# Attention and mixture-of-experts layer on one core: the stores of expert block results issued by SyncE instead of ScalarE

## The reference

```python
# x: 16 x 512 x 256
x = layernorm(x + attention(x))          # 16 heads of 16, rotary positions, ALiBi bias, softmax over 512 keys
shared = silu(X @ sW1 + sb1) @ sW2 + sb2
activation = sqrt(softplus(X @ routing_W.T + expert_bias))   # 8 experts
top_vals, top_idx = top_k(activation, 2)
y[e] = silu(X @ rW1[e] + rb1[e]) @ rW2[e] + rb2[e]           # hidden width 128
x = layernorm(x + shared + sum over the 2 chosen e of top_val * y[e])
```

## Time and profile before

| what | value |
|---|---|
| time, median of three runs | 1673.09 us (1669.12 to 1676.26) |
| the profiled execution's own time | 1669.12 us |
| its span, first to last instruction | 1667.3 us |
| granted TensorE clock, mean | 0.937 of full speed |
| busy: PE, DVE, ACT, POOL | 1458.2, 1173.1, 1018.0, 724.0 us |
| stores of block results | 77, first at 636.6 us, last at 1529.0 us |

### The profile page before, as it was taken

The page is one execution under the profiler, slowest core; times in us unless marked ns, Lnnn a source line. Parts: engine busy times, 40 slices in busy tenths (PEclk is TensorE's granted clock), DMA queues, the critical chain, the costliest instruction groups (busy, mean ns, idle before and its releaser), DMA issues.

```text
span 1667.3 us, 33130 instructions
## 1 busy us (share of the span) xinstructions
PE 1458.2 (87%) x11110; PEld 801.1 (48%) x11110; DVE 1173.1 (70%) x2631; ACT 1018.0 (61%) x1742; POOL 724.0 (43%) x655
## 2 busy tenths in 40 slices
PE   8888999999999988999989999998888888887467
PEld 4433444444444434554545544454455555564345
DVE  7765788877878786666666777768776567645584
ACT  1465666676766655767676666665566676675232
POOL 2233363554535354433425353625366343245730
PEclk8898999999999988999999999999999999998788
DMA  7444243434334243454545343444557566676531
GB/s 207 129 122 137 81 135 106 134 102 121 118 114 124 93 128 121 148 170 145 161 144 186 104 124 97 140 147 135 177 178 231 179 203 193 197 233 216 169 106 51
DMA packets 185349, 242.00 MB, mean 145 GB/s; under 512 B 67239, under 2 KB 104190, under 8 KB 185182
## 3 DMA queue, kind: packets, MB, share of 16 engines
q1 hardware_dynamic: 162138, 188.52, 37.5%
q0 software_dynamic: 10752, 29.37, 5.5%
q10 hardware_dynamic: 12292, 21.99, 3.7%
HBM read 152.53 MB, written 91.44 MB: 146 GB/s over the span
## 4 chain that ended last, share of the span: by engine, by line
PE 49%; SPq 18%; DVE 13%; DMA 11%; issue 6%; POOL 2%; ACT 1%; POOLq 0%; ACTq 0%; DVEq 0%
PE pS L644 13%; PE pV L686 9%; PE pG L710 5%; DVE negm L935 5%; SPq L390 3%; DMA d_rec<-scr 3%; PE pG L719 3%; DMA xg<-d_x 3%; PE pG L732 2%; SPq L459 2%; PE pG L821 2%; PE pG L813 2%; PE pS L650 2%; SPq L484 2%; SPq L393 2%
## 5 line engine op out<-in xcount | busy, mean ns | idle before, releaser
L935 DVE TENSOR_REDUCE negm<-pS 128x1 f32<-128x512 f32 x1024 | 659.1, 683 | 329.8 <-PE pS L650 323.2
L1371 ACT ACTIVATE ee<-pT,slp 128x512 f32<-128x512 f32 x1024 | 648.4, 684 | 213.5 <-PE pT L671 210.3
L644 PE MATMUL pS<-ka,qa 62*128 62x512 f32 x1024 | 480.0, 504 | 80.5 <-DVE negm L935 67.5
L665 PE MATMUL pT<-qa,ka 64*128 64x512 f32 x1024 | 477.7, 501 | 0.2 <-ACT ee L1371 0.2
L644 PEld LDWEIGHTS pS<-ka,qa 62*128 62x128 f32 x1024 | 196.8, 192 | 328.9 <-issue 312.9
L686 PE MATMUL pV<-ee,vv 128*32 128x512 f32 (+1 forms) x2048 | 288.0, 635 | 0.0
L650 PE MATMUL pS<-mAB,tri 64*128 64x64 bf16 x2048 | 242.3, 200 | 0.0
L671 PE MATMUL pT<-mAB,tri 64*128 64x64 bf16 x2048 | 239.1, 198 | 0.0
L1555 POOL TENSOR_TENSOR raw<-raw,rope 128x512 f32<-128x512 f32 x61 | 78.3, 1283 | 326.6 <-DVE sh L969 326.5
L665 PEld LDWEIGHTS pT<-qa,ka 64*128 64x128 f32 x1024 | 194.6, 190 | 4.7 <-issue 3.3
L650 PEld LDWEIGHTS pS<-mAB,tri 64*128 64x128 bf16 x2048 | 119.0, 99 | 136.9 <-issue 103.8
(11 more groups left out here) (186 smaller groups left out, 2227.3 us busy)
## 6 DMA issues: line engine op xcount, KB each, us to landing
d_part<-parts SPq DMA_DIRECT2D x63, 512.0 KB, 2.9
qa<-d_part SPq DMA_DIRECT2D x378, 64.0 KB
wb<-in_wb SPq DMA_DIRECT2D x77, 256.5 KB
xg<-d_x SPq DMA_DIRECT2D x77, 256.0 KB, 2.8
d_y<-yb ACTq DMA_DIRECT2D x77, 256.0 KB, 3.2
ka<-d_part SPq DMA_DIRECT2D x128, 128.0 KB
xT<-in_xT SPq DMA_DIRECT2D x16, 512.0 KB, 4.0
ka<-d_part SPq DMA_DIRECT2D x128, 64.0 KB
```

What stands on the lines that cost most here:

```text
L644: e.matmul(pS[:, k, :], qa[g % 4][r, i, t * 128:t * 128 + 128].bitcast(F32R), ka[g % 4][r, i, :].bitcast(F32R), start=True, stop=False)
L665: e.matmul(pT[:, k, :], ka[g % 4][r, i, kt * 128:kt * 128 + 128].bitcast(F32R), qa[g % 4][r, i, :].bitcast(F32R), start=True, stop=False)
L935: e.tensor_reduce(negm[:, g % 2, j, t + k:t + k + 1], pS[:, k, :], AX, ALU.max, negate=True).then_inc(s_max, 1)
L1371: e.activation(ee[:, k, d % 7, :], pT[:, k, :], ACT.Exp, scale=slp[:, 6, h:h + 1]).then_inc(s_exp, 1)
```

## The change

`store_block` moves from ACT's program to SP's, unchanged. In a step, SP issues it behind the loads of a block and ahead of the writes of rotated queries and keys; ACT issued it behind the two exponentials and ahead of everything else. The step (B+4), the wait for the copy, the tile and the count of landings stay.

```diff
@@ SyncE's program
+        def store_block(q):
+            g = GROUP_OF_BLOCK[q]
+            j = q - FIRST_BLOCK[g]
+            e.wait_ge(g_free[bk("downb", 0, q)], full("downb", 0, q))
+            e.dma_start(d_y[g][j * ROWS:(j + 1) * ROWS, :].rearrange("(p k) c -> p k c", k=2), yb[q % 3][:, :, :]
+                        ).then_inc(y_w[q % 3], 16)
...
             for q in LOAD_BLOCKS.get(s, ()):
                 load_block(q)
+            if (q := block_due(s, STOREB)) >= 0:
+                store_block(q)
@@ ScalarE's program
-        def store_block(q):
-            g = GROUP_OF_BLOCK[q]
-            j = q - FIRST_BLOCK[g]
-            e.wait_ge(g_free[bk("downb", 0, q)], full("downb", 0, q))
-            e.dma_start(d_y[g][j * ROWS:(j + 1) * ROWS, :].rearrange("(p k) c -> p k c", k=2), yb[q % 3][:, :, :]
-                        ).then_inc(y_w[q % 3], 16)
...
             if 0 <= s - LAG < NC:
                 exps(s - LAG)
-            if (q := block_due(s, STOREB)) >= 0:
-                store_block(q)
```

## The result

The changed kernel takes 1682.95 us, the median of twelve (1677.53 to 1693.48). The kernel before, run twelve times beside it, takes 1670.86 (1661.7 to 1676.26). The ratio is 1.0083, with a 95% interval of 1.0055 to 1.0111: slower by 0.8%, about 14 us. (The quotient of these two medians is 1.0072, or 12 us; the ratios of this document are the recorded ones, and the two ways of counting differ by up to 0.2%.) The forecast was 1683.5 and +0.6%.

A forecast was written before the change was run, and what follows sets the result against it. PE leads the chain with 49%, SyncE's queue holds 18%, ACT 1%. 0 from ACT + 8.0 for issues + 2.4 for queueing = +10.4 us on the median 1673.09: 1683.5 us, +0.6%, range 1673 to 1698.

The forecast's parts named there:

- ACT gets back nothing: On ACT, a store's 0.33 us of queue is covered by the running 0.67 us exponential, so 0 is gained.
- SP pays 0.40 us for an issue: On SP's queue, each moved store takes 0.40 us, priced from SP's own plain write of a tile.
- 20 places on the chain, 8.0 us: Of 77 stores, 20 fall where the chain runs through SP, four in 744-850 us, sixteen later: 8.0 us.
- the second rival: SP's slack runs out, so every store counts: bound +40 us, case +20, 1693 us; chance 0.16.
- The queue, 2.4 us: Stores ahead of three reciprocal writes, and the last store behind an output write, delay landings 0 to 1.2 us each: 2.4.
- Later stores, 0: SP's later stores delay group 1's first gather and the reuse of store tiles: cost 0, at most about 1 us.
- The store's line is on the chain: Sign: the store's line appears on the chain some twenty times at about 0.4 us.
- SPq's share: Sign: the share of the chain held by SyncE's queue rises from 18%.
- PE's wait for tokens: Sign: PE's wait for a block's tokens grows from 49.3 us by roughly the sum; 20 us or more means slack ran out.
- The waits for DVE in the first stretch: Sign: SP's waits for DVE between 640 and 940 us, its slack there, shrink.
- Relief (3): SP's round trips from 1195 to 1530 us shorten, 21.6 us back: -13.6, 1659.5 us; chance 0.07 shared with ACT being held.
- Paid back (1): Loads and round trips on the chain land sooner, 4.1 us back, no queue term: +3.9, 1677 us; chance 0.33.

The follow-up runs named there:

- experiment 1: Against the kernel before, an unused register read added at each of the 77 store places: on SP ratio 1.0109, on ACT 0.9978.
- Experiment 8: Against the kernel before, ACT also issues softmax-sum writes, outputs, the weight row's read and loads of weights and bias: 1665.94 against 1683.27 us, ratio 0.9899.
- Group 0 alone: SP issues only the 31 stores of group 0, ACT the others; against the kernel before 1686.79 against 1683.27 us, ratio 1.0045.
- experiment 5: Stores split between SP and ACT, against the kernel before: SP with group 0 (31 stores) ratio 1.0045, SP with groups 1 and 2 (46) ratio 1.0110.
- experiment 3: Kernel before, stores still on ACT but two steps later for the first 55 blocks and one step later for the rest: ratio 0.9978.

## Why the prediction was right, point by point

- **Sign and size: right.** +0.6% was forecast, +0.83% and +0.86% measured. That 1683.5 us is only 0.5 from the measured 1682.95 is luck: the median of before that I started from lies 2.2 us above that of twelve, and the step that I added is 2 to 4 us too small.
- **ACT gets back nothing: confirmed.** The starts are unchanged, and 0.45 us more per place on ACT's queue costs nothing measurable (experiment 1). Experiment 8 shows the condition: it holds while what the queue does fits under the running exponentials.
- **SP pays 0.40 us for an issue: confirmed** by the fences above (0.40 to 0.46). That SP's time alone is enough for such a loss is shown by the register read, which moves nothing; scaled to 0.40 us it gives 0.6% of the 0.83%.
- **20 places on the chain, 8.0 us: the term that was mis-sized.** The two profiles have 29 and 34, 14.0 and 14.5 us. I had laid the stores onto the chain of before; but where PE led with SP close behind, the added 0.40 us can let SP take the lead. That is my reading of the extra places, and it is the second rival's mechanism, at about a third of its bound of 40 us: SP's waits for DVE and ACT held enough slack for the rest. The prediction counted only the two waits for DVE in the first stretch and overlooked the 23.7 us for ACT. Of the stores on the chain 9 and 5 are in group 0 and 20 and 29 behind it, against four and sixteen. Group 0 alone showed +0.45%, some 7.6 us, against 1.6 predicted, but its interval goes down to 0.11%.
- **The queue, 2.4 us: too much.** Of its four places one shows up: the last store lands 0.8 and 0.9 us later than in the earlier trace rows, between my bounds of 0 and 1.2. The Trainium skill (DMA: Bandwidth & Descriptors, section "Queues, rings and completion order") says that a ring's descriptors are consumed in order; by my bound that would be up to 1.2 there. The reciprocals' round trips are not longer (1.9 and 2.0 us a time against 1.9). So the trace agrees with that rule at the end at most, and doesn't show it elsewhere. The two errors, 6 us too little for the places and 1.5 too much for the queue, offset each other in part. 14.0 + 0.9 is near the 14 us measured, but this leaves no room for the few us that go with the clock, and experiment 5 shows how far pieces on the chain and loss can part; that they agree so well is partly luck.
- **Later stores, 0: confirmed** (experiment 3). In the changed kernel the first gather of group 1 starts at 1483.27, behind 11.33 us of waiting for the store issued at 1479.88; DVE first uses its rows at 1489.05. From gather to use it is 5.8 us, where it was 11.4 in the earlier trace rows: the gather comes 5.6 us later against its use, much as I had worked out (my 1460.6 should read 1460.5). DVE's only wait for a gather near it is 0.86 us, at 1500.25, and the kernel before has one of 0.87 at 1477.12.
- **What would show it.** The store's line is on the chain as said, with more places. SPq's share rose, but by less than it scatters between kernels that lost nothing (14 to 18%), and the register read, at 1.1% slower, has 18% as before: a poor sign. PE's wait for tokens did not: it is 50.6 us in the first profile (49.3 before) and 59.5 in the second. Profiles of kernels no slower than before have 33.5 (experiment 3) and 40.1 (the read on ACT), so this number scatters by more than the effect, and I should not have named it as a test of a 10 us step. The waits for DVE in the first stretch (640 to 940 us) are 15.9 us before, 11.5 and 16.3 after, so they did not clearly shrink either. They shrank only over the whole of 640 to 1560 us.
- **Rivals.** Relief (3) is out, since the result is slower. Its sign was a bad one, though: in the crowded stretch (1195 to 1282 us) the round trips did fall, from 3.8 us a time to 2.6 in both profiles and from 1.9 to 1.3 and 1.1. But these are two or three waits each, and the kernels with a single small write and with the register read on SP, whose stores are on ACT, have 3.0 and 2.2, and 1.3 and 1.3, so the stores' queue need not be what made them shorter. Paid back (1) is out by the interval, whose lower end is +0.55%. The slack running out (2) is there in part, as said.
- **Open:** whether the 0.2% beyond the proportion of experiment 1 is the queue's or scatter; what part of the loss goes through the clock; and why a small write on SP costs no more than one on ACT.

## What to carry to other kernels

In this kernel an issue that moved cost above all its queue time, and that was free where it was hidden: on ScalarE under an instruction that still runs, on SyncE inside a wait that it would sit out anyway. Before moving issues, read both covers, and count not only the places where the receiving queue is on the chain but also those where it is close behind. When the queue named in the chain is one that only issues, look for issues to take off it: 80 fewer, together with a shorter wait behind the write of the sums, gave 2.2% here. The limit was reached when a register read and three issues in a row, 2.2 us of ScalarE's queue, outlasted 1.25 us of exponentials.

## What the runs showed that I had not expected

- 77 writes of 2 KB in 16 B pieces cost 1.7% and 1.9%, about 0.4 us each, on either engine, where moving 77 issues of 256 KB to the queue that bounds the kernel costs 0.8%. PE's granted clock was lower and its busy time 22 to 31 us longer in them. The cause was not found.
- One register read on SyncE takes 0.64 us of its queue, more than a DMA issue (0.35). On ScalarE it takes 0.45.
- The same kernel scatters by 1%, and the granted clock goes with it: the read on ACT took 1654.31 us at 0.946 and 1672.03 at 0.936. Two chips differ by 0.8% in the kernel before. Hence two profiles can't be subtracted for an effect of this size; ratios on one chip can.
